# First projection, pattern projections and pattern values: split operands in three passes in place of plain 32-bit products

## The reference, cut to what matters

```
h = layernorm(x)                          # (1024, 256)
q_mid = rmsnorm(h @ q_a_w.T) ; kv_a = h @ kv_a_w.T ; gates = softmax(h @ gate_w.T + gate_b)
pq = split_heads(h @ sp_q_w.T) ; pk = split_heads(h @ sp_k_w.T) ; pv = split_heads(h @ sp_v_w.T)
p_probs = softmax(pq @ pk.T / 4) ; p_ctx = p_probs @ pv
```

## Time and profile before

| | us |
|---|---|
| median of 3 runs | 809.86 |
| lowest, highest | 809.43, 809.92 |
| the profiled execution's time | 808.8 |
| its span in the trace | 807.0 |
| PE busy in the span | 759.7 |
| DVE busy | 582.3 |
| POOL busy | 430.3 |
| ACT busy | 392.0 |

### The profile page before, as it was taken

How to read it: one execution, slowest core, us unless ns; L and a number is a source line. 1 busy time by engine, 2 the same in 40 slices (tenths; PEclk the granted TensorE clock), 3 DMA queues, 4 the chain that set the end, 5 groups by cost and what they waited for, 6 DMA issues and landing times. The chain is left out here.

```text
span 807.0 us, 13734 instructions
## 1 busy us (share of the span) xinstructions
PE 759.7 (94%) x5408; PEld 472.2 (59%) x5408; DVE 582.3 (72%) x672; ACT 392.0 (49%) x492; POOL 430.3 (53%) x259
## 2 busy tenths in 40 slices
PE   5998889999999999999999999999999998989894
PEld 5764556655665565656555655655556554458773
DVE  5876646765779677857775788677767799974846
ACT  3632445555455555555555555455555554530361
POOL 1443049544954594368437852865296745450233
PEclk9999999999999999999999999999999999999987
DMA  9895571026202620363044105420535103302001
GB/s 238 293 264 201 130 133 27 1 73 107 61 1 60 112 79 2 74 110 95 2 117 96 40 1 107 90 56 14 102 66 169 35 28 126 125 2 85 1 1 52
DMA packets 97796, 68.13 MB, mean 84 GB/s; under 512 B 66434, under 2 KB 76228, under 8 KB 97476
## 3 DMA queue, kind: packets, MB, share of 16 engines
q1 hardware_dynamic: 97732, 67.25, 33.3%
HBM read 41.23 MB, written 17.04 MB: 72 GB/s over the span
## 5 line engine op out<-in xcount | busy, mean ns | idle before, releaser
L1011 POOL TENSOR_TENSOR acc<-acc,em 128x1024 f32<-128x1024 f32 x96 | 237.3, 2472 | 53.5 <-ACT em L1068 50.6
L1154 DVE TENSOR_REDUCE m2p<-xb 128x2 f32<-128x1024 f32 x128 | 156.0, 1222 | 74.0 <-PE xb L1312 74.0
L1162 DVE TENSOR_REDUCE m<-xb 128x2 f32<-128x1024 f32 x128 | 155.7, 1218 | 54.2 <-PE xb L1312 53.9
L1059 ACT ACTIVATE ep<-xb 128x1024 f32<-128x1024 f32 x128 | 131.3, 1026 | 116.0 <-PE xb L1312 115.9
L1068 ACT ACTIVATE em<-xb 128x1024 f32<-128x1024 f32 x128 | 131.1, 1024 | 95.2 <-PE xb L1312 90.9
L1348 PE MATMUL pvm<-em,cpair 128*32 128x512 f32 x1024 | 136.9, 607 | 0.0
L974 POOL TENSOR_TENSOR rot<-rot,sin 128x512 f32<-128x512 f32 x32 | 41.2, 1289 | 131.3 <-DMA rot<-raw 131.3
L1312 PEld LDWEIGHTS xb<-pq,pk 49*128 49x128 f32 x256 | 24.0, 184 | 108.6 <-issue 98.5
L1011 POOL TENSOR_TENSOR acc<-em 128x1024 f32<-128x1024 f32 x16 | 38.2, 2387 | 79.5 <-PE xb L1463 67.3
L1359 PE MATMUL pvp<-ep,vp 128*32 128x512 f32 x512 | 66.7, 592 | 0.0
L1312 PE MATMUL xb<-pq,pk 49*128 49x512 f32 x256 | 64.4, 499 | 1.3 <-issue 1.3
(11 more groups left out here) (277 smaller groups left out, 1268.9 us busy)
## 6 DMA issues: line engine op xcount, KB each, us to landing
rot<-raw SPq DMA_DIRECT2D x128, 64.0 KB, 2.5
pk<-spqk_d SPq DMA_DIRECT2D x48, 128.0 KB, 4.2
sums<-rec_d SPq DMA_DIRECT2D x32, 128.0 KB, 2.9
ctx_d<-ctxr SPq DMA_DIRECT2D x14, 256.0 KB, 2.1
pq<-spqk_d SPq DMA_DIRECT2D x48, 64.0 KB, 2.4
wraw<-wst_d SPq DMA_DIRECT2D x7, 384.0 KB, 6.0
em<-in_o_w SPq DMA_DIRECT2D x1, 2048.0 KB, 7.6
vp<-vp_d SPq DMA_DIRECT2D x8, 256.0 KB, 5.1
```

Source lines behind the costliest of these rows:

```text
L1011: pool.tensor_tensor(acc[:, :, :], before, em[:, j:j + 2, :], ALU.add).then_inc(added, 1)
L1059: act.activation(ep[:, j:j + 2, :], src[:, :, :], ACT.Exp, scale=PAT_SCALE).then_inc(ep_ready, 1)
L1154: dve.tensor_reduce(m2p[:, 2 * tp:2 * tp + 2, t, kt], src[:, :, :], AX, ALU.max).then_inc(x_dve, 1)
L1162: dve.tensor_reduce(m2[:, q, :, t, kt], src[:, :, :], AX, ALU.max).then_inc(x_dve, 1)
```

## The change

Three kinds of product go from plain F32 to split operands: `proj1`, the eight pattern projections (`spqk`, `sk`), and the pattern values (`sv`). For that, `w1T`, `xT` and `spT` become split jobs: ACT writes hi, DVE writes lo. The separate making of `xh`, `xl` by ACT and POOL falls away with its two semaphores, and the F32 tile `xT` too; its memory (`work`) holds the lo parts of the pattern weights. Four of the eight `proj1` tiles (the odd ones) are now evacuated by ACT. `("P", 2)` waits for the evacuation of the last `xT` job in place of `xh_ready` and `xl_ready`.

```diff
-    split = ("spqk", "cT", "qm0T", "qm1T")
-    act_jobs = [("w1T", 0), ("w1T", 1), ("xT", 0, 0), ("xT", 1, 0), ("spT", 0), ("xT", 1, 1), ("spT", 1), ("kpT", 0, 1),
-                ("spT", 2), ("pe1T", 0), ("lat1", 0), ("pe0T", 1), ("pe1T", 1), ("lat1", 1)]
+    split = ("w1T", "xT", "spT", "spqk", "cT", "qm0T", "qm1T")
+    act_jobs = [("proj1", t) for t in range(1, NT, 2)]
+    act_jobs += [("kpT", 0, 1), ("pe1T", 0), ("lat1", 0), ("pe0T", 1), ("pe1T", 1), ("lat1", 1)]
...
-        w1T = sb("w1T", [P, NK, W1])
+        w1h = sb("w1h", [P, NK, W1], F32R)
+        w1l = sb("w1l", [P, NK, W1], F32R)
...
-                if q == 0:
-                    evacuated(pool, index[("xT", 1, 1)])
-                pool.wait_ge(xh_ready, q + 1)
-                pool.tensor_tensor(g["xl"][:, q, :], xT[:, q, :], g["xh"][:, q, :].bitcast(F32),
-                                   ALU.subtract).then_inc(xl_ready, 1)
...
-                    for k in range(NK):
-                        mm = pe.matmul(out[:, 0:W1], xT[:, k, t], w1T[:, k, :], start=(k == 0), stop=(k == NK - 1))
-                    mm.then_inc(pe_job, 1)
+                    passes(out[:, 0:W1], [pair for k in range(NK) for pair in (
+                        (xh[:, k, t], w1h[:, k, :]), (xh[:, k, t], w1l[:, k, :]), (xl[:, k, t], w1h[:, k, :]))]).then_inc(pe_job, 1)
...
-                    for k in range(NK):
-                        mm = pe.matmul(out[:, :], spT[w][:, k, 0:P], xT[:, k, half_of(h)],
-                                       start=(k == 0), stop=(k == NK - 1))
-                    mm.then_inc(pe_job, 1)
+                    passes(out[:, :], [pair for k in range(NK) for pair in (
+                        (sph[w][:, k, 0:P], xh[:, k, half_of(h)]), (spl[w][:, k, 0:P], xh[:, k, half_of(h)]),
+                        (sph[w][:, k, 0:P], xl[:, k, half_of(h)]))]).then_inc(pe_job, 1)
...
-                if job in (("proj1", 3), ("proj1", 7)):
-                    k = job[1] // 4
-                    evacuated(act, index[("xT", k, 1)])
-                    act.activation(g["xh"][:, k, :], xT[:, k, :], ACT.Copy).then_inc(xh_ready, 1)
...
+                    dve.tensor_tensor(lo, src, hi.bitcast(F32), ALU.subtract).then_inc(ev_dve, 1)
...
-                            pe.wait_ge(done["xh_ready"], 2)
-                            pe.wait_ge(done["xl_ready"], 2)
+                            done["evacuated"](pe, done["index"][("xT", 1, 1)])
...
-                    mm = passes(out[:, 0, :], [(spT[w][:, k, m * P:(m + 1) * P], xT[:, k, half_of(h)])
-                                               for k in range(NK)])
+                    xh, xl = (g[n][:, :, half_of(h)] for n in ("xh", "xl"))
+                    rows = slice(m * P, (m + 1) * P)
+                    mm = passes(out[:, 0, :], [pair for k in range(NK) for pair in (
+                        (sph[w][:, k, rows], xh[:, k, :]), (spl[w][:, k, rows], xh[:, k, :]), (sph[w][:, k, rows], xl[:, k, :]))])
...
-                        mm = passes(out[:, 0, j * HID:(j + 1) * HID],
-                                    [(xT[:, k, t * P:(t + 1) * P], spT[2][:, k, :]) for k in range(NK)])
+                        xh, xl = (g[n][:, :, t * P:(t + 1) * P] for n in ("xh", "xl"))
+                        mm = passes(out[:, 0, j * HID:(j + 1) * HID], [pair for k in range(NK) for pair in (
+                            (xh[:, k, :], sph[2][:, k, :]), (xh[:, k, :], spl[2][:, k, :]), (xl[:, k, :], sph[2][:, k, :]))])
```

More of the change, by code:

```diff
@@ L112, in prologue @@
         hi_ready = sem("hi_ready")
-        xh_ready = sem("xh_ready")
-        xl_ready = sem("xl_ready")
         lstat = sem("lstat")
@@ L225, in transposes, with passes @@
                 mm.then_inc(pe_job, 1)
+            def passes(out, pairs):
+                for n, (w, x) in enumerate(pairs):
+                    mm = pe.matmul(out, w, x, start=(n == 0), stop=(n == len(pairs) - 1))
+                return mm
             pe.wait_ge(s_ident, 16)
@@ L293, in plain @@
             kind, out = job[0], bank[n % 8]
-            if kind == "xT":
-                return xT[:, job[1], half_of(job[2])], out[:, :]
-            if kind == "w1T":
-                return w1T[:, job[1], :], out[:, 0:W1]
             if kind == "proj1":
                 return m1[:, job[1], :], out[:, 0:W1]
-            if kind == "spT":
-                return spT[job[1]].rearrange("p k n -> p (k n)"), out[:, :]
             q = job[-1]
@@ L304, in plain, with hi_lo_of @@
             return wall[q][:, :, c, :], out[:, :].rearrange("p (n j) -> p n j", j=P)
-        def hi_of(job):
-            if job[0] == "spqk":
-                return sp_stage(job)[0]
-            return g[{"cT": "kyh", "qm0T": "qm0h", "qm1T": "qm1"}[job[0]]][:, half_of(job[1])]
+        def hi_lo_of(n):
+            job = jobs[n]
+            kind, out = job[0], bank[n % 8][:, :]
+            if kind == "w1T":
+                return w1h[:, job[1], :], w1l[:, job[1], :], out[:, 0:W1]
+            if kind == "xT":
+                return xh[:, job[1], half_of(job[2])], xl[:, job[1], half_of(job[2])], out
+            if kind == "spT":
+                return tuple(t[job[1]].rearrange("p k n -> p (k n)") for t in (sph, spl)) + (out,)
+            if kind == "spqk":
+                return sp_stage(job) + (out,)
+            half = half_of(job[1])
+            if kind == "qm1T":
+                return g["qm1"][:, half], g["qm1"][64:P, half], out
+            return tuple(g[t][:, half] for t in (("kyh", "kyl") if kind == "cT" else ("qm0h", "qm0l"))) + (out,)
         def scalar_program(act):
@@ L431, in pattern_weights @@
 def pattern_weights(g):
-    flat = [g["kxl_f"][:, 1, 0:HALF], g["kxl_f"][:, 1, HALF:S], g["kxh_f"][:, 1, 0:HALF]]
-    return [t.rearrange("p (k n) -> p k n", n=HID) for t in flat]
+    hi = [g["kxl"][:, 1, 0:HALF], g["kxl"][:, 1, HALF:S], g["kxh"][:, 1, 0:HALF]]
+    lo = [g["work"][:, 0, 0:HALF], g["work"][:, 0, HALF:S], g["work"][:, 1, 0:HALF]]
+    return tuple([t.rearrange("p (k n) -> p k n", n=HID) for t in some] for some in (hi, lo))
 ORDER = [0, 2, 3, 1]
```

25 lines of the change are left out of this document (11 added, 14 removed).

## The result

The changed kernel takes 806.34 us (median of 16 runs, 804.98 to 808.88), against 808.25 us for the kernel before on the same chip (16 runs, 804.83 to 810.23): a ratio of 0.9972, 95% interval 0.9959 to 0.9986. It is faster by 0.28%, some 2.3 us by this ratio (1.9 us between the two medians). I had forecast 1.1 us less and "no change that a measurement can tell"; the time lies under my range of 807.0 to 811.9. The median of three runs that I started from, 809.86, lay 1.6 us above that of the 16.

A forecast was written before the change was run, and what follows sets the result against it. The prediction took DVE, then SP's queue, then PE and DVE in turn as bounds up to slot 0's end; -0.5 us (prologue) and -0.6 (slot 0) made -1.1, median 809.86 to 808.8 us, range 807.0 to 811.9.

The forecast's parts named there:

- What bounds the kernel: Start to end of slot 0: DVE up to 42 us, SP from 43 to 72, then PE and DVE alternating.
- The price of a pass: PE's split passes of 256 columns: 0.122 us each, so proj1 0.73 us a tile and sv 1.46.
- Rival A: PE's split tiles: weight loads not hidden at 256 columns, so slower, 812.0 us; chance 0.12.
- The prologue: Up to the first P tile: +0.4 and +0.6 us of DVE work, -1.55 of gaps, sum -0.5 us.
- rival B: Prologue: queues of ACT and DVE lose what PE gains, an ACT pair 1.7 us; 809.7 us, chance 0.25.
- D: Early prologue: w1T's lo parts wait for DVE's normalisation and push proj1, 0.8 us more; 809.9 us, chance 0.05.
- nobody on the path waited for POOL: Prologue: POOL loses two subtractions, which no one on the path waited for, so no gain was counted.
- Slot 0: Slot 0: sk0 to sk3 and sv0 to sv2 gain 0; sk4 and sv3 behind 71.86 us together -0.6 us.
- SP's chain starts 0.5 us earlier, and what follows up to 71.86 with it: SP's queue, first turn to first mm tile: the prologue's 0.5 us passes through whole.
- store of 6.34 us: SP's queue between 43 and 66.90 us: one store alone holds it for 6.34 us.
- Rival C: More shifts, such as oT0's wait, the clock and later slots: 807.8 us or 809.8; chance 0.2 for the fast side.
- The regular slots: Behind slot 0: the tiles are the old ones and shift as a whole, so no gain or loss there.

The follow-up runs named there:

- b_pad48: The kernel before with 48 idle 32x32 transposes on PE ahead of the first oT tile; 809.93 us, ratio 1.0.
- a_plain_sv: The changed kernel with the four sv tiles as plain 32-bit products of the hi parts alone; 812.74 us, ratio 1.0035.
- sv_pad16: The kernel of a_plain_sv with 16 idle 32x32 transposes on PE ahead of the first oT tile; 806.66 us, ratio 0.9953.

## Why the prediction was off, point by point

**What bounds the kernel: right.** DVE up to 40 us, SP from 43 to 72, then PE and DVE. Plain passes in the prologue moved the first turn, SP's new order shortened the piece from the turn to the mm tile, and PE's sv tiles mattered behind 72 us, each as named.

**The price of a pass: right.** Forecast 0.122 us for 256 columns and 0.73 us for a proj1 tile; the rows above give 0.12 and (17.64 - 14.68) / 4 = 0.74. spqk ran at 24.61 - 23.24 = 1.37 us. sv3 took 78.33 - 76.70 = 1.63 us and not 1.46, since its first pass and the step to the next tile take 0.2 us each in place of 0.12; it made no difference, since DVE was the limit there. Rival A falls: the load of the weights hides at 256 columns too, and the loads even overlap one another, as one is shown with 0.19 us and the next starts 0.12 us after it. The Trainium skill has both sides of it: the rule of TensorE: Matmul & The Clock Gate, Part 3, "The mechanism", which I weighed, and in Part 2, "Step-by-step: what each phase is for", the load that is pulled ahead into a background buffer. The trace agrees with the latter.

**The prologue: right in kind, a term missing.** In the profiled pair the statistics came 0.42 us later (0.4 forecast) and both gaps went. That agreement is luck: over the ten and the six executions the statistics start at 22.9 us on average after and 23.0 before, so the 0.4 us is not there, and of the 1.55 us of gaps some 0.3 remain. An ACT pair took 22.57 - 21.24 = 1.33 us (1.47 forecast), so rival B falls, and PE started proj1 at 14.5 us on average in both kernels, so D does too. The sum was short because of one sentence: "nobody on the path waited for POOL". No semaphore did, but DVE's addition was held by POOL's subtraction for 0.59 us (it starts at 23.86 in the stretch of the earlier trace rows, between two of the rows shown there; I took its 0.73 us for its own length). -0.5 and -0.6 make the -1.17 us that the first qm1T shows in the pair (-1.4 on average).

**Slot 0: half right.** Behind the first mm tile the gain was 0.60 us, as forecast (8.04 to 7.44). The step that failed is "SP's chain starts 0.5 us earlier, and what follows up to 71.86 with it": 1.07 us at the first turn were 0.86 at the third key's turn and 0.31 at the mm tile. The DMA engines are full there (a share of 1.05 between 60 and 66 us), and an earlier issue need not land earlier; that is my reading of the rows, and no run isolates it. The prediction's store of 6.34 us is part of the same misreading: in the new order the hold stays and the store doesn't have it. Rival C named the clock. It goes with the two forms of slot 0 that the kernel before has: where the half clock falls before 68 us, the piece from the first turn to slot 1 takes 56.31 us, and where it falls behind the first mm tile, 57.92. The changed kernel was of the first kind in all its profiles (56.46, 56.18, and 56.19 with POOL's subtractions back), with a wait of 3.6 to 4.5 us at oT0 and the dip behind it. So part of the gain between medians may be this, up to 1.6 us in an execution; how often the kernel before takes the second form I can't tell from two profiles.

**The regular slots: wrong.** "From there on the tiles are the old ones and shift as a whole" is the step that failed, and the largest: -2.17 us of -3.09. The tiles are the old ones, but the place where instruction blocks land depends on PE's program, and they collide with SP's stack loads or don't. b_pad48, which has the changed kernel's length and the old work, has 634.90 us there; a_plain_sv and sv_pad16 differ by length alone, and by 6 us of median. That this is a matter of where blocks land is shown for the waits for the stack; for the rest of those microseconds only the length is shown to matter. The -2.17 us is the pair's; what the medians leave for this piece is an estimate of 1 us or so, 2.3 less the prologue's and sv's share below.

**The base.** Three runs gave 809.86 with 0.5 us between them; in the six comparisons of this study the kernel before had medians of 808.25 to 809.98, with single runs from 804.8 up. I should have held 1 to 1.5 us of spread in the base itself against a forecast of 1.1.

What would hold without luck: -1.4 us from the prologue and -0.6 from sv, about 2 us, less up to 0.8 that SP's queue takes back. The rest isn't the change's own work.

## What to carry to other kernels

When a queue of DMA issues or a full set of DMA engines sets the end, reorder that queue first: it gave 6 us here where faster products gave 2 to 3, and on top of it they gave nothing measurable. Where PE gets faster and its savings run together into one idle time, look at the granted clock behind it: a wait of 2.9 us cost 2.6 us of work behind it. And before a gain or loss under 1% is put down to an edit, run the old kernel with idle instructions up to the new length.

## What the runs showed of the hardware

- Length of PE's program alone: 14 tiny idle transposes took the kernel from 803.06 to 805.28 us, and 16 took another from 812.74 to 806.66. Where a q8 block lands on them, six DMA issues of SP take 3.3 to 4.8 us in place of 2.77, in 19 of 19 cases.
- SP's queue: behind two large loads the next issue takes 6.3 to 6.6 us, whichever it is: a store in one order (0.38 us in the other), a small load in the other (0.51 us in the first).
- DVE and POOL: an addition of 128x16 with both inputs in SBUF took 0.14 us alone, and 0.73 and 1.02 us beside a subtraction on POOL, up to the end of that one.
- The granted clock behind idle time: it was 0.50 after 2.94 us and after 3.62 us of waiting, 1.00 throughout with the wait of 2.94 us filled by transposes whose result nobody reads (0.54 us left). Behind waits of 1.5 to 2.15 us both outcomes occur.
- A split pass of 256 columns with new weights each time: 0.12 us, though a weight load is shown with 0.19. With 512 columns: 0.43 us at the granted clock of 0.50, 0.23 at 1.00.
